# A graph layer on one core: message sums in plain fp32 over windows of 64 nodes, and VectorE adds the gathered rows and b_e in place of a stored table and ScalarE copies

## The chip, the cores and the metric

One core of a Trainium2 chip runs the whole kernel. The metric is the device time of a run in microseconds (us). The profile is one profiled execution of the same program.

## What is computed

A graph has 8192 nodes with 256 features (x) and 131072 edges with 64 attributes, sorted by destination. The parts that matter here:

```
ea  = edge_attr @ w_e + b_e                      # 131072 x 256
msg = relu(x[src] + ea)                          # rows of x gathered by src
agg = segment_sum(msg, dst, num_segments=8192)
h_local = relu((x + agg) @ w1 + b1) @ w2 + b2    # then a scale, a shift and a residual
attention over graphs of 32 nodes, 4 heads; out = h_local + h_attn
out = out + relu(out @ m_w1 + m_b1) @ m_w2 + m_b2; a layer norm ends it
```

## The kernel before, in words

**Turns.** The 131072 edges are 1024 tiles of 128; two tiles are a pair (512 pairs), four pairs a group (128 groups of 1024 edges). A turn handles two pairs, so there are 256 turns and three more at the end; eight turns, with four groups, go with one block of 256 nodes. Each of the engines PE (TensorE), DVE (VectorE), ACT (ScalarE), POOL (GpSimd) and SP (which issues most DMAs) has its own program, written out by hand turn by turn, with waits on semaphores between them; every engine works strictly in the order of its program. `heads_in` and `nodes_in` say which step of which block's attention and node layers falls into which turn.

**Gathers (L316 to L335).** POOL issues two indirect DMAs for each pair, 1024 in all. Each takes 128 indices from the SBUF tile `srcs` and brings 128 rows of 1 KB into `xg`, which has room for 8 pairs (NX). For the first 80 pairs (XB_PAIR) the rows come from x, and POOL may go as far as seven pairs are already copied (`s_seed`). From then on they come from `xb_dram`, a table of x + b_e, and POOL waits once every two pairs for the edge products (`s_prod`) of the turn three back. The table is made during the first 32 turns: SP loads a sixteenth of x, DVE adds b_e to it (`add_be`, L565, instruction at L569), and SP stores it.

**A pair's way.** ACT copies the two gathered tiles into one of four PSUM banks `EA` (`seed`, L354, copy at L360), after their landing (`s_xg`) and after the bank is free. PE adds the edge attributes times w_e on top (`products`, L728, matmuls at L746: 64 rows each, two pairs side by side in the two halves of the array's rows); for the first 80 pairs it also adds b_e by a matmul of ones with b_e split in two fp32r parts (L738). ACT makes the high half of the message, relu rounded to fp32r (`high`, L362, at L364); DVE makes the low half, relu minus the high half (`low`, L559, at L561).

**A group's way.** DVE makes a 128x128 0/1 matrix for each of the eight tiles of a group (`make_onehot`, L572, at L573): which of 128 nodes from the group's first one an edge goes to. PE multiplies it with both halves of the messages, 16 fp32r matmuls into bank `G` (`sum_group`, L752, at L761). ACT copies the sums out (`copy_agg`, L369), PE transposes them (L770), and DVE adds them to a window of 128 nodes in `aggT` (`add_agg`, L579, at L591). The window's start is loaded from `base_i` into a register.

**Order.** DVE's turn is: `low` of two pairs, in even turns `add_agg`, `add_be` and `make_onehot`, then attention and node steps. ACT's turn is: `seed` of the next turn's two pairs, `high` of this turn's, in odd turns `copy_agg`, then attention and node steps. PE's turn is `products`, in odd turns `sum_group`, in even turns the transposes, then attention and node steps (all plain matmuls of the dense layers are at L710). In two turns of eight a node step of DVE (L635, L653) waits for a product that PE makes late in the same turn. Other two-input additions and products of DVE on SBUF tiles are L618 and L677, in attention and in the layer norm.

Of the kernel before, what the change touches and what calls it, by code (L numbers as in the profile page):

```python
# [16 lines left out]
P = 128  # L17
TG = 8
# [13 lines left out]
XB = 16  # L32
XB_ROWS = N // XB // P
XB_PAIR = XB * PG + 16
# [3 lines left out]
PER = N // NG  # L38

# [24 lines left out]

EA_PE = XB_PAIR // PG + 1

# [18 lines left out]
def gnn_layer(nc, t, out):  # L86
# [5 lines left out]
    k.xb_dram = nc.dram_tensor("xb_dram", (N, C), fp32, kind="Internal").ap()  # L92
    with ExitStack() as ctx:
# [10 lines left out]
        k.ident, k.iota = sb("ident", [P, P]), sb("iota", [P, P])  # L104
# [5 lines left out]
        k.base_i, k.bad_i = sb("base_i", [P, P], i32), sb("bad_i", [P, 1], i32)  # L110
        k.lohi = sb("lohi", [P, 6])
# [4 lines left out]
        k.be_rows, k.be_hl = sb("be_rows", [P, C]), sb("be_hl", [P, C], f32r)  # L116
        k.be_ones = sb("be_ones", [P, P], f32r)
        k.xrow = sb("xrow", [P, 2, XB_ROWS, C])
# [6 lines left out]
        k.mh, k.ml = sb("mh", [P, NM, 2 * C], f32r), sb("ml", [P, NM, 2 * C], f32r)  # L125
        k.onehot = sb("onehot", [P, 2, TG, P], f32r)
# [26 lines left out]
def program(nc, k):  # L153
    t, EA, G, X = k.t, k.EA, k.G, k.X
    aggT, ident, vecT, s12 = k.aggT, k.ident, k.vecT, k.s12
    xg, ea, mh, ml, onehot = k.xg, k.ea, k.mh, k.ml, k.onehot
    with ExitStack() as ctx:
        def sem(name):
# [8 lines left out]
        s_xrow = [sem(f"s_x_part_{n}") for n in range(2)]  # L167
        s_xadd, s_xbst = sem("s_be_added"), [sem(f"s_xb_stored_{n}") for n in range(2)]
# [8 lines left out]
        s_be = sem("s_be_split")  # L177
        s_seed, s_prod, s_mh, s_ml = (sem(n) for n in ("s_x_seeded", "s_ea_product", "s_msg_high",
                                                       "s_msg_low"))
        s_seg, s_agg, s_aggT, s_added = (sem(n) for n in (  # L180
            "s_group_summed", "s_agg_copied", "s_agg_transposed", "s_agg_added"))
        s_oh = sem("s_onehot_made")
# [36 lines left out]
        def _(sp):  # L219
# [27 lines left out]

            xb_parts = k.xb_dram.rearrange("(m p r) c -> m p r c", p=P, r=XB_ROWS)
            x_parts = t["x"].rearrange("(m p r) c -> m p r c", p=P, r=XB_ROWS)

            def load_part(m):
                if m >= 2:
                    sp.wait_ge(s_xbst[m % 2], 16 * (m // 2))
                sp.dma_start(k.xrow[:, m % 2, :, :], x_parts[m, :, :, :]).then_inc(s_xrow[m % 2], 16)

            for m in range(2):
                load_part(m)
            for turn in range(TURNS):
# [3 lines left out]
                m = turn // 2  # L262
# [4 lines left out]
                if turn % 2 == 1 and 2 <= m + 1 < XB:  # L267
                    load_part(m + 1)
# [37 lines left out]
        def _(pool):  # L306
# [9 lines left out]
            for q in range(NP):  # L316
# [946 lines left out]
```

## Time and profile before

| | us |
|---|---|
| runs of the kernel before, median of 2 | 1602.03 (1601.25 to 1602.81) |
| profiled execution, first to last instruction (span) | 1362.1 |
| PE busy, of the span | 1284.3 |
| POOL busy, of the span | 982.0 |
| DVE busy, of the span | 860.7 |
| ACT busy, of the span | 804.9 |

The profile gives the profiled execution's span and no other time of it; the runs' median lies 239.9 us above that span. Busy times leave out register, branch, semaphore and DMA-issuing instructions, except that a gather on POOL counts as busy while POOL builds it. A fp32 matmul of the program stands as two instructions in the trace, an fp32r one as one.

### The profile page before, as it was taken

The page shows a single profiled execution, that of the slowest core. Times are in us where ns is not written, and L with a number is a line of the kernel's source. Part 1 is how long each engine was busy: PE and PEld are TensorE (multiplying, and loading weights), DVE is VectorE, ACT ScalarE, POOL GpSimd, SP SyncE. Part 2 cuts the span into 40 slices and gives each one's busy share as a digit, 9 for nine tenths or more (in the row PEclk, how much of TensorE's full clock was granted, in tenths as well). Part 3 has the DMA queues.
Part 4 walks back from the last instruction along what each step waited for, and adds up shares of the span by engine and source line. Part 5 has one row for each costly group of instructions (what it writes and reads, how often), then busy time and mean ns, then how long its engine had stood idle before and what let it go on. Part 6 is the DMA issues. An engine that isn't in the chain of part 4 may idle for free.

```text
span 1362.1 us, 22937 instructions
## 1 busy us (share of the span) xinstructions
PE 1284.3 (94%) x8410; PEld 1045.5 (77%) x8410; DVE 860.7 (63%) x1690; ACT 804.9 (59%) x1697; POOL 982.0 (72%) x1032
## 2 busy tenths in 40 slices
PE   5988999999999999999999999999999999999997
PEld 4777888777877777777777787777777777778776
DVE  3786676666566566566666666666666666566642
ACT  2555555665566566666666666666666666666652
POOL 7777774777777777777777777777777777777750
PEclk8999999999999999999999999999999999999999
DMA  9777764556445555545555545555554555554441
GB/s 345 237 242 248 238 215 126 170 167 174 141 146 171 174 163 174 157 131 170 175 170 171 167 143 154 175 174 167 175 158 138 168 175 172 169 161 148 138 120 32
DMA packets 109651, 232.93 MB, mean 171 GB/s; under 512 B 21985, under 2 KB 46817, under 8 KB 109537
## 3 DMA queue, kind: packets, MB, share of 16 engines
q0 software_dynamic: 49152, 134.28, 34.6%
q1 hardware_dynamic: 58944, 93.87, 20.5%
q10 hardware_dynamic: 1440, 3.29, 0.7%
q8 instruction: 67, 1.10, 0.3%
q14 instruction: 48, 0.39, 0.1%
HBM read 206.19 MB, written 25.17 MB: 170 GB/s over the span
## 4 chain that ended last, share of the span: by engine, by line
POOL 51%; PE 21%; issue 17%; DVE 6%; DMA 3%; ACT 1%; SPq 0%; DVEq 0%; POOLq 0%; ACTq 0%
POOL xg L331 51%; PE bank L761 5%; PE bank L710 5%; PE both L710 5%; PE bank L746 4%; DMA xg<-xb_dram,srcs 2%; DVE onehot L573 2%; DVE ml L561 1%; DMA aggT<-in_xT_dram 1%; DVE xrow L569 1%; PE bank L738 1%; ACT mh L364 1%; PE bank L849 1%; DVE aggT L591 0%; PE both L886 0%
## 5 line engine op out<-in xcount | busy, mean ns | idle before, releaser
L331 POOL DMA_INDIRECT xg<-xb_dram,srcs x864 | 820.4, 950 | 283.5 <-issue 258.3
L561 DVE SCALAR_TENSOR_TENSOR ml<-bank,mh 128x512 fp32r<-128x512 f32 x512 | 329.8, 686 | 308.3 <-ACT mh L364 305.7
L360 ACT COPY bank<-xg 128x512 f32<-128x512 f32 x512 | 301.5, 597 | 210.0 <-DMA xg<-xb_dram,srcs 167.7
L364 ACT ACTIVATE mh<-bank 128x512 fp32r<-128x512 f32 x512 | 277.5, 594 | 162.1 <-PE bank L746 160.5
L761 PE MATMUL bank<-mh,onehot 128*128 128x256 f32 x1024 | 266.2, 298 | 52.0 <-DVE onehot L573 52.0
L746 PE MATMUL bank<-we,ea 64*128 64x256 f32 x2048 | 290.0, 402 | 0.0
L761 PEld LDWEIGHTS bank<-mh,onehot 128*128 128x128 f32 x1024 | 196.7, 192 | 97.1 <-DVE onehot L573 77.5
L761 PE MATMUL bank<-ml,onehot 128*128 128x256 f32 x1024 | 253.1, 285 | 0.0
L746 PEld LDWEIGHTS bank<-we,ea 64*128 64x128 f32 x2048 | 177.7, 187 | 74.3 <-issue 30.3
L331 POOL DMA_INDIRECT xg<-in_x_dram,srcs x160 | 160.6, 1004 | 51.7 <-issue 43.6
L761 PEld LDWEIGHTS bank<-ml,onehot 128*128 128x128 f32 x1024 | 197.4, 193 | 0.0
L573 DVE TENSOR_TENSOR onehot<-bank,rel 128x1024 fp32r<-128x1024 f32 x128 | 155.6, 1215 | 0.0
L369 ACT COPY agg<-bank 128x256 f32<-128x256 f32 x128 | 47.7, 373 | 135.4 <-PE bank L761 135.4
L710 PE MATMUL both<-xT,iwT 128*128 128x256 f32 x512 | 123.8, 385 | 0.0
L710 PE MATMUL both<-m,h 128*128 128x256 f32 x496 | 117.3, 379 | 0.0
L710 PEld LDWEIGHTS both<-xT,iwT 128*128 128x128 f32 x512 | 92.4, 190 | 15.7 <-issue 5.0
L710 PEld LDWEIGHTS both<-m,h 128*128 128x128 f32 x496 | 89.5, 190 | 9.6
L635 DVE SCALAR_TENSOR_TENSOR h<-xT,s,bank 128x256 f32<-128x256 f32 x64 | 27.9, 477 | 108.5 <-PE bank L710 108.5
L710 PE MATMUL bank<-h,m 128*128 128x256 f32 x264 | 64.7, 389 | 1.7 <-DVE h L635 1.7
L710 PE MATMUL bank<-oT,owT 128*128 128x256 f32 x256 | 65.7, 379 | 0.0
L710 PE MATMUL bank<-h,w 128*128 128x256 f32 x256 | 65.5, 379 | 0.0
L710 PE MATMUL both<-iwT,xT 128*128 128x256 f32 x240 | 62.7, 384 | 0.0
(111 smaller groups left out, 1402.6 us busy)
## 6 DMA issues: line engine op xcount, KB each, us to landing
ea<-in_ea_dram SPq DMA_DIRECT2D x128, 256.0 KB, 3.9
xg<-xb_dram,srcs POOLq DMA_INDIRECT x864, 2.8
xT<-in_xT_dram SPq DMA_DIRECT2D x32, 256.0 KB, 3.6
aggT<-in_xT_dram SPq DMA_DIRECT2D x32, 256.0 KB
xrow<-in_x_dram SPq DMA_DIRECT2D x16, 512.0 KB, 6.3
xb_dram<-xrow SPq DMA_DIRECT2D x16, 512.0 KB, 3.2
oT_dram<-oT SPq DMA_DIRECT2D x32, 256.0 KB, 2.5
xn<-in_x_dram SPq DMA_DIRECT2D x32, 256.0 KB, 4.6
```

The source lines that it names most:

```text
L331: pool.indirect_dma_start(xg[:, q % NX, n * C:(n + 1) * C], None, t["x"] if q < XB_PAIR else k.xb_dram[:, :], bass.IndirectOffsetOnAxis(k. ...
L360: nc.scalar.copy(EA[q % 4][:, :], xg[:, q % NX, :]).then_inc(s_seed, 1)
L364: nc.scalar.activation(mh[:, q % NM, :], EA[q % 4][:, :], ACT.Relu).then_inc(s_mh, 1)
L369: nc.scalar.copy(k.agg[:, :], G[:, 0:C]).then_inc(s_agg, 1)
L561: nc.vector.scalar_tensor_tensor(ml[:, q % NM, :], EA[q % 4][:, :], 0.0, mh[:, q % NM, :].bitcast(fp32), ALU.max, ALU.subtract).then_inc(s ...
L569: nc.vector.tensor_tensor(part, k.be_rows[:, :].unsqueeze(1).to_broadcast([P, XB_ROWS, C]), part, ALU.add).then_inc(s_xadd, 1)
L573: nc.vector.tensor_tensor(onehot[:, n % 2, :, :], G[:, 2 * P:3 * P].unsqueeze(1).to_broadcast([P, TG, P]), k.rel[:, n, :].unsqueeze(2).to_ ...
L635: ins = nc.vector.scalar_tensor_tensor(k.o[:, c, :], k.xT[:, j % NXT, c, :], s12[:, 6 + c:7 + c], B[:, c * NB:(c + 1) * NB], ALU.mult, ALU ...
L710: ins = nc.tensor.matmul(to, stationary(c), moving(c), start=start and c == 0, stop=stop and c == blocks - 1, skip_group_check=skip)
L738: nc.tensor.matmul(EA[(2 * d + tile // 2) % 4][:, tile % 2 * C:(tile % 2 + 1) * C], k.be_ones[:, :], k.be_hl[:, :], start=False, stop=True ...
L746: ins = nc.tensor.matmul(EA[(2 * d + pair) % 4][:, two * C:(two + 1) * C], ea[rows, n % NEA, at:at + P], k.we[rows, :], start=False, stop= ...
L761: ins = nc.tensor.matmul(G[:, 0:C], onehot[:, n % 2, tile, :], half[:, q % NM, two * C:(two + 1) * C], start=tile == 0 and half is mh, sto ...
```

## The change

It takes out the table `xb_dram`, its loads, stores and additions, the split of b_e and its matmuls, and ACT's copies. DVE now adds gathered rows and b_e into the PSUM bank for all pairs, at the start of its turn. The message is one plain fp32 tile made by ACT. The sums are plain fp32 over windows of 64 nodes: a group's first four tiles go to the upper half of `G`, the last four to the lower half, each half with a window start of its own, and `add_agg` adds them one after the other. All gathers read x, and POOL waits by `s_prod` from the ninth pair on.

```diff
-XB = 16
-XB_ROWS = N // XB // P
-XB_PAIR = XB * PG + 16
+SUB = 2
+TS = TG // SUB
+W = P // SUB
...
-        k.mh, k.ml = sb("mh", [P, NM, 2 * C], f32r), sb("ml", [P, NM, 2 * C], f32r)
-        k.onehot = sb("onehot", [P, 2, TG, P], f32r)
+        k.msg = sb("msg", [P, NM, 2 * C])
+        k.onehot = sb("onehot", [P, 2, TG, W])
...
@@ POOL @@
-                if q == XB_PAIR:
-                    for n in range(2):
-                        pool.wait_ge(s_xbst[n], 16 * (XB // 2))
-                if NX <= q < XB_PAIR:
-                    pool.wait_ge(s_seed, q - NX + 1)
-                if q >= XB_PAIR and q % 2 == 0:
-
+                if q >= NX and q % 2 == 0:
                     pool.wait_ge(s_prod, q // 2 - 2)
...
-                        t["x"] if q < XB_PAIR else k.xb_dram[:, :],
+                        t["x"],
@@ ACT @@
-            def seed(q):
-                act.wait_ge(s_xg[q % NX], 32 * (q // NX + 1))
...
-                nc.scalar.copy(EA[q % 4][:, :], xg[:, q % NX, :]).then_inc(s_seed, 1)
-
-            def high(q):
+            def message(q):
                 act.wait_ge(s_prod, q // 2 + 1)
-                nc.scalar.activation(mh[:, q % NM, :], EA[q % 4][:, :], ACT.Relu
-                                     ).then_inc(s_mh, 1)
+                nc.scalar.activation(msg[:, q % NM, :], EA[q % 4][:, :], ACT.Relu
+                                     ).then_inc(s_msg, 1)
@@ DVE @@
-            def low(q):
...
-            def add_be(n):
...
+            def seed(q):
+                dve.wait_ge(s_xg[q % NX], 32 * (q // NX + 1))
+                if q == 0:
+                    dve.wait_ge(s_ber, 16)
+                    dve.wait_ge(s_set, 1)
+                if q >= 4:
+                    dve.wait_ge(s_msg, q - 3)
                 nc.vector.tensor_tensor(
-                    part, k.be_rows[:, :].unsqueeze(1).to_broadcast([P, XB_ROWS, C]), part, ALU.add).then_inc(s_xadd, 1)
+                    EA[q % 4][:, :].rearrange("p (a c) -> p a c", a=2),
+                    xg[:, q % NX, :].rearrange("p (a c) -> p a c", a=2),
+                    k.be_rows[:, :].unsqueeze(1).to_broadcast([P, 2, C]), ALU.add
+                ).then_inc(s_seed, 1)
...
             def add_agg(n):
-                at = nc.vector.value_load(k.base_i[0:1, n:n + 1], min_val=0, max_val=N - P)
+                at = [nc.vector.value_load(k.base_i[0:1, sub, n:n + 1], min_val=0, max_val=N - W)
+                      for sub in range(SUB)]
                 dve.wait_ge(s_aggT, n + 1)
-                if n == NG - 1:
+                if n:
                     dve.wait_ge(s_added, n)
...
+                sums = G[:, 0:C].rearrange("p (c n) -> p c n", n=P)
+                for sub in range(SUB):
+                    if sub:
+                        dve.wait_ge(s_half, n + 1)
+                    window = aggT[:, :, bass.ds(at[sub], W)]
+                    nc.vector.tensor_tensor(window, sums[:, :, sub * W:(sub + 1) * W], window,
+                                            ALU.add).then_inc(s_added if sub else s_half, 1)
...
-            add_be(0)
+            seed(0)
+            seed(1)
             make_onehot(0)
...
-                for q in (a, b):
+                for q in (a + 2, b + 2):
                     if q < NP:
-                        low(q)
+                        seed(q)
@@ PE @@
-                if 2 * d < XB_PAIR:
-                    for tile in range(4):
-                        nc.tensor.matmul(
-                            EA[(2 * d + tile // 2) % 4][:, tile % 2 * C:(tile % 2 + 1) * C],
-                            k.be_ones[:, :], k.be_hl[:, :], start=False, stop=True,
-                            skip_group_check=True)
...
             def sum_group(n):
-                if n == NG - 1:
-                    pe.wait_ge(s_ml, NP)
+                pe.wait_ge(s_msg, PG * (n + 1))
+                if n < NG - 1:
+                    pe.wait_ge(s_oh, n + 2)
+                else:
                     pe.wait_ge(s_added, n)
-                else:
-                    pe.wait_ge(s_oh, n + 2)
-                for tile in range(TG):
-                    q, two = PG * n + tile // 2, tile % 2
-                    for half in (mh, ml):
-                        ins = nc.tensor.matmul(G[:, 0:C], onehot[:, n % 2, tile, :],
-                                               half[:, q % NM, two * C:(two + 1) * C],
-                                               start=tile == 0 and half is mh,
-                                               stop=tile == TG - 1 and half is ml)
+                for tile in range(TS):
+                    for sub in range(SUB):
+                        at = sub * TS + tile
+                        q, two = PG * n + at // 2, at % 2
+                        ins = nc.tensor.matmul(G[sub * W:(sub + 1) * W, 0:C],
+                                               onehot[:, n % 2, at, :],
+                                               msg[:, q % NM, two * C:(two + 1) * C],
+                                               start=tile == 0, stop=tile == TS - 1)
```

The set-up on DVE loses the split of b_e and works out two window starts for each group in place of one; the softmax step 7 on DVE waits for ACT's exponentials in every block instead of the last one alone.

## Rows read from the trace of the kernel before

**Rows 1.** The page: an engine's busy time, and PE's granted clock in 40 slices.

```profile
PE 1284.3 (94%) x8410; PEld 1045.5 (77%) x8410; DVE 860.7 (63%) x1690; ACT 804.9 (59%) x1697; POOL 982.0 (72%) x1032
...
PEclk8999999999999999999999999999999999999999
```

**Rows 2.** The page: the chain that ended last, by engine.

```profile
POOL 51%; PE 21%; issue 17%; DVE 6%; DMA 3%; ACT 1%; SPq 0%; DVEq 0%; POOLq 0%; ACTq 0%
```

**Rows 3.** Waits of POOL: us in total, times, longest us.

```profile
POOL xg L331 <- PE bank L746: 25.1, 17, 11.9
POOL xg L331 <- ACT bank L360: 6.5, 16, 1.7
```

**Rows 4.** Groups of gathers: count, busy us, mean ns of one, idle before.

```profile
L331 POOL DMA_INDIRECT xg<-xb_dram,srcs x864 | 820.4, 950 | 283.5 <-issue 258.3 <-PE bank L746 25.1
...
L331 POOL DMA_INDIRECT xg<-in_x_dram,srcs x160 | 160.6, 1004 | 51.7 <-issue 43.6 <-ACT bank L360 6.5 <-DMA srcs<-in_srcs_dram 1.5
```

**Rows 5.** Timeline of POOL, first and last gathers: start us, duration us.

```profile
3.37 1.18 POOL L331 DMA_INDIRECT xg<-in_x_dram,srcs  x1 [1.53 <-DMA srcs<-in_srcs_dram]
4.86 0.95 POOL L331 DMA_INDIRECT xg<-in_x_dram,srcs  x1 [0.30 <-issue]
...
27.40 1.99 POOL L331 DMA_INDIRECT xg<-in_x_dram,srcs  x1 [0.30 <-issue]
...
1317.04 0.95 POOL L331 DMA_INDIRECT xg<-xb_dram,srcs  x1 [0.30 <-issue]
```

**Rows 6.** One block of eight turns by windows: length; PE, PEld, DVE, ACT, POOL busy; clock.

```profile
655.97:695.93 39.96, 38.77 (x257) 31.34 (x257) 25.96 (x52) 25.16 (x53) 30.46 (x32) 1.00 0.56 163
```

**Rows 7.** Timelines of gathers (POOL) and VectorE instructions that overlap them.

```profile
124.38 1.22 DVE L569 TENSOR_TENSOR xrow<-be_rows,xrow 128x1024 f32<-128x1024 f32 x1
124.58 1.84 POOL L331 DMA_INDIRECT xg<-in_x_dram,srcs  x1 [0.30 <-issue]
...
306.42 0.42 DVE L618 TENSOR_TENSOR dif<-dif,rs 128x256 f32<-128x256 f32 x1
306.55 1.11 POOL L331 DMA_INDIRECT xg<-xb_dram,srcs  x1 [0.30 <-issue]
...
652.09 1.21 DVE L573 TENSOR_TENSOR onehot<-bank,rel 128x1024 fp32r<-128x1024 f32 x1
652.19 0.95 POOL L331 DMA_INDIRECT xg<-xb_dram,srcs  x1 [0.30 <-issue]
```

**Rows 8.** Groups of VectorE: count, busy us, mean ns of one.

```profile
L561 DVE SCALAR_TENSOR_TENSOR ml<-bank,mh 128x512 fp32r<-128x512 f32 x512 | 329.8, 686 | 308.3 <-ACT mh L364 305.7
...
L573 DVE TENSOR_TENSOR onehot<-bank,rel 128x1024 fp32r<-128x1024 f32 x128 | 155.6, 1215 | 0.0
...
L591 DVE TENSOR_TENSOR aggT<-bank,aggT 128x256 f32 x128 | 54.4, 425 | 9.0 <-PE bank L770 6.6 <-issue 1.9
```

**Rows 9.** ACT's copies (L360) and what they waited for; gathers, issue to landing.

```profile
L360 ACT COPY bank<-xg x512: 576/590/632, 11.5 to 1321.2; 128x512 f32<-128x512 f32 x171
...
  DMA xg<-xb_dram,srcs: 167.7, 159
...
  DMA xg<-in_x_dram,srcs: 14.4, 4
...
xg<-xb_dram,srcs POOLq DMA_INDIRECT x864, 2.8
```

**Rows 10.** PE: timeline of one block, and the group of the b_e matmuls.

```profile
650.05 2.76 PE L710 MATMUL both<-xT,iwT 128*128 128x256 f32 x12
...
686.23 0.28 PE L761 MATMUL bank<-mh,onehot 128*128 128x256 f32 x1
686.35 0.28 PE L761 MATMUL bank<-ml,onehot 128*128 128x256 f32 x1
686.56 1.09 PE L849 MATMUL bank<-probT,vn 128*64 128x128 f32 x16
...
L738 PE MATMUL bank<-be_hl,be_ones 128*128 128x256 f32 x160 | 33.5, 334 | 13.5 <-ACT bank L360 13.5
```

More of the change, by code:

```diff
@@ L466, in settle @@
                 dve.wait_ge(s_own, made[0])
-            lo, hi, base, bad, span, off = (k.lohi[:, n:n + 1] for n in range(6))
+            lo, hi, base, bad, span, off = (k.lohi[:, n, :] for n in range(6))
+            even = k.even[:, 0:1].to_broadcast([P, SUB])
             dve.wait_ge(s_ident, 4)
-            step_of(nc.vector.tensor_copy(G[:, 2 * P:3 * P], k.iota[:, :]))
-            nc.vector.tensor_scalar(k.be_ones[:, :], ident[:, :], 0.0, None, ALU.mult)
+            step_of(nc.vector.tensor_copy(G[:, 2 * P:2 * P + W], k.iota[:, :]))
@@ L489, in _ @@
             settle()
             nc.vector.tensor_tensor(span, hi, base, ALU.subtract)
-            nc.vector.tensor_tensor(bad, lo, k.even[:, :], ALU.subtract)
-            step_of(nc.vector.tensor_tensor(off, base, k.even[:, :], ALU.subtract))
+            nc.vector.tensor_tensor(bad, lo, even, ALU.subtract)
+            step_of(nc.vector.tensor_tensor(off, base, even, ALU.subtract))
             settle()
-            nc.vector.tensor_scalar(span, span, float(P - 1), None, ALU.is_gt)
+            nc.vector.tensor_scalar(span, span, float(W - 1), None, ALU.is_gt)
@@ L495, in _ @@
             nc.vector.tensor_scalar(bad, bad, float(-PER * SLACK), None, ALU.is_lt)
-            step_of(nc.vector.tensor_scalar(off, off, float(AHEAD * NB - (GI - 1) * PER - P), None,
+            step_of(nc.vector.tensor_scalar(off, off, float(AHEAD * NB - (GI - 1) * PER - W), None,
                                             ALU.is_gt))
             settle()
-            step_of(nc.vector.tensor_tensor(bad, bad, span, ALU.max))
+            step_of(nc.vector.tensor_reduce(
+                k.bad[:, :], k.lohi[:, 3:6, :].rearrange("p a s -> p (a s)"), AX.X, ALU.max))
@@ L508, in _ @@
-            step_of(nc.vector.tensor_reduce(span, X[0][:, P:2 * P], AX.X, ALU.max))
+            for sub in range(SUB):
+                tiles = slice(sub * TS, (sub + 1) * TS)
+                ins = nc.vector.tensor_tensor(
+                    k.rel[:, :, tiles], k.dst_p[:, :, tiles],
+                    X[0][:, sub * P:(sub + 1) * P].unsqueeze(2).to_broadcast([P, NG, TS]),
+                    ALU.subtract)
+            step_of(ins)
+            nc.vector.tensor_copy(k.base_i[:, :, :].rearrange("p s n -> p (s n)"),
+                                  X[0][:, 0:SUB * P])
```

113 lines of the change are left out of this document (28 added, 85 removed).

## The prediction

> **What bounds the kernel now.** I read the page's busy shares first. PE is busy for 1284.3 us of 1362.1, at nearly full clock (2.4 GHz) but for the first slice [rows 1], and looks like the bound. The chain that ended last says otherwise: 51% of it is POOL, and a further 17% "issue", time between instructions [rows 2]. So I looked at POOL's gathers. There are 1024, each takes 0.95 us, and the next one starts 0.30 us after it although nothing is waited for; from 4.86 to 27.40 us there are 18 starts in a row, one every 1.252 us [rows 4, 5]. At that pace 1024 gathers need 1023 x 1.252 + 0.95 = 1282 us. The first starts at 3.37 and the last ends at 1317.99 us [rows 5], a stretch of 1314.6 us. The 32.6 us above the pace are: 25.1 + 6.5 us of waits for PE and ACT in 33 places, less the 33 x 0.30 us that are pace anyway, so 21.7 us [rows 3]; (1004 - 950) ns x 160 = 8.6 us of longer gathers in the first part [rows 4]; and 2.3 us scattered. After the last gather come 44.1 us of tail. POOL's queue of gathers is the bound, and at most 22 us can come from whatever POOL waits for. PE is the close second: a block of eight turns, 32 gathers, lasts 39.96 us, and PE is busy in 38.77 of them [rows 6].
>
> **Why some gathers are long** is the second thing to read, in the timelines [rows 7]. A gather that started at 124.58 took 1.84 us instead of 0.95. It started inside the addition of b_e at L569, which has two inputs in SBUF and ended at 125.60; the gather ended at 126.42, 0.82 later. The same at 306.55: the softmax product L618, two SBUF inputs too, ended at 306.84, and the gather at 307.66, again 0.82 later. The gather at 27.40 (1.99 us [rows 5]) is of this kind. The control is the gather at 652.19, inside a one-hot comparison that reads one input from PSUM and one from SBUF: 0.95 us, undisturbed. So about 0.13 us after its start a gather does something (0.95 - 0.82) that must wait until a two-SBUF-input instruction of DVE has ended.
>
> **Pricing that.** If such an instruction of length L stands at an arbitrary place in a pitch T of 1.25 us, it delays the gathers by L x L / 2T on average. For L569: 1.22 x 1.22 / 2.5 = 0.60 us each; the measured cost is 8.6 us over 16 additions, 0.54 us each. The formula holds to a tenth.
>
> **The change, part by part.**
> 1. DVE's new `seed` adds xg and be_rows, both in SBUF, 128x512, into PSUM, 512 times. The trace has no such shape; the 128x512 instruction at L561 takes 0.686 us [rows 8], and L569 with twice the elements 1.22 us, so I take 0.69. By the formula a seed at an arbitrary place costs the gathers 0.69 x 0.69 / 2.5 = 0.190 us. But a seed that waits for its rows is not at an arbitrary place: the rows land 2.8 us after the issue of the pair's second gather [rows 9], that is 0.3 us into the third pitch after it, past the sensitive 0.13 us, and the seed ends at 0.99, before the next start at 1.25. Those cost nothing. How many wait? ACT's copies, which stand at the same place of ACT's turn, did so 159 + 4 times of 512 [rows 9]; the other 349 came late. I take the same share: 349 x 0.190 = 66 us on POOL's path. Bounds: none delayed, 0; all at arbitrary places, 512 x 0.190 = 97 us.
> 2. The waits of POOL, 21.7 us, mostly go: the additions of b_e by PE (33.5 us busy for 160 instructions [rows 10]) leave the first 40 turns, where PE was the slower one, and the change of wait rule at pair 80, the single wait of 11.9 us [rows 3], no longer falls there. The stricter rule now holds from pair 8, and can cost at the start; I leave 5 us of waits, between 0 and 12.
> 3. The 16 additions at L569 go, and with them 8.6 us of long gathers.
> 4. Sums on PE. Sixteen fp32r matmuls follow each other at 0.12 us: 1.92 us a group. A plain fp32 one of the same size is two instructions of 0.216 us each ((2.76 - 0.38) / 11, twelve in a row). The eight new ones, 16 instructions, would be 3.46 us in a row. But they alternate between the halves of the output partitions as L849's do, and there 16 instructions of 128 columns took (1.09 - 0.28) / 15 = 0.054 us each, half of the 0.108 that such a stream needs alone [rows 10]. So 16 x 0.108 = 1.73 us; 0.2 us a group comes off PE, 0.8 of the 38.77 us of a block. It is hidden behind POOL: worth nothing but some 1 us in the tail.
> 5. DVE: 512 seeds for 512 `low` of the same length; the one-hot halves from 1.215 to about 0.69 us; the window addition of 0.425 us [rows 8] becomes two, each between 0.21 and 0.42, with a second register load and a wait between. Together DVE is some 0.2 us a group lighter. Off the path. ACT loses 512 copies of 0.59 us. Off the path as well, as are 32 transfers of 512 KB.
> 6. DVE is in order: in two turns of eight it stands before a product of PE (node steps at L635 and L653) and the next turn's seeds are queued behind it, so PE's next products but one wait. Written out over one block with these durations, PE's work is 38.0 us and about 1 us of waiting comes in; POOL's 40 us cover it. If the gathers were not there, it would be the bound.
>
> **A page against the change.** The Trainium skill, SBUF - State Buffer, "Who interferes with whom", says that a DVE instruction with two SBUF inputs contends with a GpSimd instruction that reads SBUF, and that the second to start blocks until the first is done. It agrees with [rows 7]: the gather reads its indices from SBUF. The same section infers that tensor_tensor does not hold up DMAs issued by GpSimd, because building descriptors needs the write interface only; by that the first term would be 0 and the time 1576 us. The 1.84 us gather speaks against it.
>
> **The sum**, against the span: start 3.4, pace 1282, scattered 2.3, seeds 66, waits 5, tail 43.1 = 1401.8 us, 39.7 us above 1362.1. The runs' median lies 239.9 us above the span; nothing in the trace says what that is, and I carry it over unchanged: 1602.0 + 39.7 = 1641.7 us, 2.5% slower. A measurement of this kernel tells about 2%, 32 us, from no change.
>
> **Rivals.** (a) Likeliest, 60%: late seeds hold up gathers, with between 40 and 95 us: 1615 to 1671 us, 1642 in the middle. (b) 25%, on the other side: the seeds hardly hold up gathers, because writing to PSUM makes them different or because nearly all of them fall in step with the landings once PE has slack. It decides from 26 us of delay downwards. With 0 to 26 us the time is 1602 - 26.3 + (0 to 26) = 1576 to 1602 us. For it: 163 copies already fell in step, and a slower POOL lets more do so. Against it: DVE has turns with over 3 us of attention work, after which its seeds are late whatever the landings do. (c) 5%: the two halves of the sum don't overlap. Then a group costs 1.54 us more, a block 38.77 + 6.2 = 45 us, and PE is the bound: 5 us x 32 - 20 = 140 us more, about 1742 us. (d) 10%: DVE's order becomes the bound, with 2 to 3 us for each block beyond POOL's pace on top of half of the delays: 1602 - 26 + 33 + 64 to 96 = 1673 to 1705 us. The clock could join in (d): with PE idle more often, stretches at the half clock (1.2 GHz) as in the first slice would appear.
>
> **How the numbers follow.** Slower by over 2% (above 1634): all of (c) and (d), and of (a)'s 0.60 some 0.42, since delays up to 58 us leave it below: 0.57. Within 2%: the other 0.18 of (a), and 0.20 of (b)'s 0.25: 0.38. Faster by over 2% (below 1570): 0.05, from (b), if the start also goes better than assumed. The range from 1580 to 1685 takes in the bounds 0 (nearly) and 97 of the seeds' delay and the nearer half of (d), and leaves out (c) and the ends.
>
> **What would show it.** Right: gathers with a mean of about 1.01 us, many of 1.1 to 1.6 us that started inside a seed and ended 0.82 us after it; hardly a wait on POOL; PE idle for 5% more of the span, waiting for seeds; sum matmuls that start every 0.108 us. Wrong: gathers of 0.95 us throughout (b); sum matmuls at 0.216 us (c); POOL waiting for PE in every block while PE waits for DVE (d); or a distance between span and median other than 240 us.

## The result and the profile after

The changed kernel takes 1575.58 us, the median of 2 runs (1575.54 to 1575.62), against 1602.03 us before. The ratio is 0.9838 with a 95% interval of 0.9808 to 0.9868: 1.6% faster. The forecast was 1642 us with a range of 1580 to 1685 us, so it had the wrong sign and the range missed.

The page of the changed kernel: busy shares and granted clock, then the chain that ended last by engine.

```profile
PE 1363.5 (87%) x8251; PEld 973.1 (62%) x8251; DVE 793.9 (50%) x1797; ACT 524.5 (33%) x1185; POOL 1025.5 (65%) x1032
...
PEclk8978999999999899999999999999999999999989
...
PE 38%; another core or an unknown queue 28%; ACT 10%; DVE 10%; issue 9%; POOL 2%; DVEq 2%; DMA 0%; SPq 0%
```

Beside [rows 1] and [rows 2] this is another regime, not the same one with a small edit. POOL had 51% of the chain before and has 2% now; 28% goes to waits whose releaser the profile cannot name. The span is 1573.9 us, only 1.7 us below the median of the runs, where it was 239.9 us below it before. Next, who waited (engine, line, waited for: us in total, times, longest), changed kernel:

```profile
ACT msg L324 <- remote: 461.0, 128, 6.1
POOL xg L299 <- issue: 273.6, 879, 1.0
POOL xg L299 <- remote: 151.4, 101, 2.3
POOL xg L299 <- PE bank L692: 71.9, 43, 3.2
```

```profile
707.83 1.14 PE L692 MATMUL bank<-we,ea 64*128 64x256 f32 x8
...
710.04 1.89 PE L662 MATMUL both<-h,m 128*128 128x256 f32 x8
...
712.21 1.08 ACT L324 ACTIVATE msg<-bank 128x512 f32<-128x512 f32 x2 [5.05 <-remote]
```

```profile
708.73 0.94 POOL L299 DMA_INDIRECT xg<-in_x_dram,srcs  x1 [0.30 <-issue]
709.97 0.95 POOL L299 DMA_INDIRECT xg<-in_x_dram,srcs  x1 [0.30 <-issue]
712.45 0.94 POOL L299 DMA_INDIRECT xg<-in_x_dram,srcs  x1 [1.53 <-remote]
```

The products end at 708.97. ACT, which needs nothing but them, begins at 712.21, 3.2 us later; POOL, which waits for the same semaphore, begins at 712.45. POOL had stopped at 710.92, and the update came 1.3 us after that. PE itself was not held up: it began further matmuls at 709.17, 710.04 and 711.86. Over all matmuls of this trace that raise a semaphore I set the time of the update against the end of the matmul, which the profile models: half of the recorded updates come more than about 2 us late, a tenth more than about 5 us. Nine tenths of the recorded updates of ACT and DVE come within 0.01 us in the same trace. In the profile of before, PE's come within 0.02 us.

So the 240 us between the profile of before and its runs were not time around the span. That profile is of an execution with PE's updates on time; the timed runs, as I infer from their times and from `e1_before` below, were of the other kind, with PE's updates late. Which kind it is seems to go with the chip: each of the first four sets of runs below was on one chip (9, 8, 5 and 11), and within a set all kernels were of one kind. The fifth was on two, 0 and 5, both of the kind with updates on time. Chip 5 is the only one that was seen twice.

### The profile page after: what moved, and what is told of

It reads as the page before. It is cut to its first block, busy times and chain, and to the rows that moved or that the text cites. A ratio compares the mean times of both kernels' runs of the same rounds, so it can differ in the third digit from the quotient of the medians.

```text
span 1573.9 us, 22965 instructions
## 1 busy us (share of the span) xinstructions
PE 1363.5 (87%) x8251; PEld 973.1 (62%) x8251; DVE 793.9 (50%) x1797; ACT 524.5 (33%) x1185; POOL 1025.5 (65%) x1032
## 4 chain that ended last, share of the span: by engine, by line
PE 38%; another core or an unknown queue 28%; ACT 10%; DVE 10%; issue 9%; POOL 2%; DVEq 2%; DMA 0%; SPq 0%
PE both L662 11%; PE bank L662 8%; PE bank L692 8%; PE bank L708 8%; ACT msg L324 5%; DVE bank L516 3%; POOL xg L299 2%; DVEq L530 2%; DVE onehot L523 1%; ACT h L333 1%; PE bank L717 1%; DVE mx L556 1%; DVE aggT L546 1%; ACT agg L329 1%
## 5 line engine op out<-in xcount | busy, mean ns | idle before, releaser
L299 POOL DMA_INDIRECT xg<-in_x_dram,srcs x1024 | 1024.5, 1001 | 498.5 <-issue 273.6
L324 ACT ACTIVATE msg<-bank 128x512 f32<-128x512 f32 x512 | 278.0, 596 | 719.5 <-remote 461.0
L692 PE MATMUL bank<-we,ea 64*128 64x256 f32 x2048 | 317.8, 418 | 92.0 <-DVE bank L516 59.0
L516 DVE TENSOR_TENSOR bank<-xg,be_rows 128x512 f32<-128x512 f32 x512 | 332.9, 695 | 64.6 <-DMA xg<-in_x_dram,srcs 36.8
L708 PE MATMUL bank<-msg,onehot 128*64 128x256 f32 x2048 | 272.8, 410 | 42.3 <-DVE onehot L523 33.1
L546 DVE TENSOR_TENSOR aggT<-bank,aggT 128x128 f32 x256 | 74.6, 291 | 371.8 <-remote 217.7
L708 PEld LDWEIGHTS bank<-msg,onehot 128*64 128x64 f32 x2048 | 157.1, 145 | 144.9 <-issue 73.8
L523 DVE TENSOR_TENSOR onehot<-bank,rel 128x512 f32<-128x512 f32 x128 | 87.1, 681 | 0.1
L717 PE MATMUL bank<-ident,agg 128*128 128x128 f32 x256 | 60.0, 319 | 27.2 <-ACT agg L329 14.4
L556 DVE TENSOR_REDUCE mx<-both 32x8 f32<-32x256 f32 x128 | 53.5, 418 | 30.8 <-remote 26.8
```

The costliest lines, as they stand in the source:

```text
L299: pool.indirect_dma_start(xg[:, q % NX, n * C:(n + 1) * C], None, t["x"], bass.IndirectOffsetOnAxis(k.srcs[:, at:at + 1], 0)).then_inc(s_x ...
L324: nc.scalar.activation(msg[:, q % NM, :], EA[q % 4][:, :], ACT.Relu).then_inc(s_msg, 1)
L516: nc.vector.tensor_tensor(EA[q % 4][:, :].rearrange("p (a c) -> p a c", a=2), xg[:, q % NX, :].rearrange("p (a c) -> p a c", a=2), k.be_ro ...
L523: nc.vector.tensor_tensor(onehot[:, n % 2, :, :], G[:, 2 * P:2 * P + W].unsqueeze(1).to_broadcast([P, TG, W]), k.rel[:, n, :].unsqueeze(2) ...
L546: nc.vector.tensor_tensor(window, sums[:, :, sub * W:(sub + 1) * W], window, ALU.add).then_inc(s_added if sub else s_half, 1)
L556: ins = nc.vector.tensor_reduce(k.mx[g, :], scores[g, :, g], AX.X, ALU.max)
```

## Experiments

### First set: is it the profile that differs, and which half of the change gains?

`e1_before` is the kernel before, unchanged. `e2_sums_alone` has the new sums and leaves table, copies and additions of b_e as before:

```diff
-                for tile in range(TG):
-                    q, two = PG * n + tile // 2, tile % 2
-                    for half in (mh, ml):
...
+                for tile in range(TS):
+                    for sub in range(SUB):
+                        at = sub * TS + tile
```

`e3_seeds_alone` is the other half: no table, no copies, DVE's seeds, and the old sums and message halves.

```diff
+                nc.vector.tensor_tensor(
+                    EA[q % 4][:, :].rearrange("p (a c) -> p a c", a=2),
+                    xg[:, q % NX, :].rearrange("p (a c) -> p a c", a=2),
+                    k.be_rows[:, :].unsqueeze(1).to_broadcast([P, 2, C]), ALU.add
...
-                nc.scalar.copy(EA[q % 4][:, :], xg[:, q % NX, :]).then_inc(s_seed, 1)
```

`e4_seed_one_sbuf_input` is the changed kernel with one SBUF input in the seed; it leaves out b_e and adds the old contents of the PSUM bank in its place:

```diff
-                    k.be_rows[:, :].unsqueeze(1).to_broadcast([P, 2, C]), ALU.add
+                    EA[q % 4][:, :].rearrange("p (a c) -> p a c", a=2), ALU.add
```

Expected:

> The kernel before, unchanged, profiled once more: its span of 1362.1 us and its median of 1602.0 us don't fit together, while the changed kernel's span (1573.9) and median (1575.6) do. Theory P (TensorE really works slower in timed executions than that one profile shows: in the profile of after, semaphores of PE come a median of 2.0 us after the modelled ends of its matmuls, in that of before 0.02 us): a new profile of before shows a span near 1600 us with such late semaphores and POOL waiting for PE in many places. Theory O (240 us lie outside the span of before, and only of before): the span is 1362 us again. Time 1602 us in both.

> The change's message sums alone (plain fp32 messages, windows of 64 nodes, no low halves on DVE); ACT's copies and the table of x + b_e stay. Theory P (TensorE is the bound in timed executions, and the new sums are a little cheaper for it): most of the gain of 26 us, 1575 to 1585 us. Theory G (POOL's gathers are the bound): no gain from the sums, 1595 to 1605 us.

> The change's seeding alone: DVE adds gathered rows and b_e into the banks for all pairs, no table, no copies by ACT; messages stay split in high and low halves, with 16 fp32r matmuls a group. DVE now makes seeds and low halves. Theory P: PE loses only the b_e matmuls of 40 turns (33.5 us busy), 1575 to 1600 us, and late gathers are hidden. Theory G: gathers held up by seeds cost 40 to 97 us less the 30 us of waits that go, 1615 to 1670 us.

> The changed kernel, but the seed's second input is the PSUM bank that it writes instead of be_rows in SBUF (so b_e is left out and the bank's old sums are added): an instruction of the same size and length with one SBUF input. Both theories: gathers of 0.95 us, no long ones but those beside L571 and L630. Theory P: the time stays within 5 us of the changed kernel's 1575.6, since the delays lie beside waits for PE. Theory G: 40 to 60 us faster.

| run | us | ratio to before, 95% | span |
|---|---|---|---|
| e1_before | 1640.64 (before: 1638.38) | 1.0025 (0.998 to 1.007) | 1627.5 |
| e2_sums_alone | 1623.53 | 0.9909 (0.9875 to 0.9944) | 1627.4 |
| e3_seeds_alone | 1592.39 | 0.9731 (0.9627 to 0.9835) | 1587.6 |
| e4_seed_one_sbuf_input | 1604.04 | 0.9802 (0.9702 to 0.9903) | 1600.1 |

The kernel before, profiled again, has a span of 1627.5 us, and the same face as the changed kernel's page (who waited, e1_before):

```profile
POOL xg L331 <- issue: 270.0, 865, 1.6
POOL xg L331 <- PE bank L746: 143.2, 78, 10.7
POOL xg L331 <- remote: 121.7, 59, 2.5
POOL xg L331 <- ACT bank L360: 61.3, 21, 7.3
```

[rows 3] had 25.1 and 6.5 us in the places of the last three rows. All kernels of this set, the unchanged one included, are slower than in the first comparison, so ratios are set against each other here, and not times; in microseconds e1, e2 and e4 lie above what was expected. The half with the seeds (and without the table) gains 2.7%, the sums alone about 1%. With one SBUF input in the seeds the long gathers are gone (0.5 us beyond 0.95 us each, over all 1024), and nothing is gained by it here: e4 is not faster than e3. The changed kernel itself is not in this set.

### Second set: order on ACT, and POOL's rule of waiting

`e5_after` is the changed kernel. `e6_copy_agg_later` tests whether ACT's order is what holds up the seeds of before, `e7_gathers_by_seed` lets POOL run on by the seeds and not by the products, `e8_seeds_alone_again` repeats e3.

```diff
-                if turn % 2 == 1 and 3 <= turn <= 2 * NG + 1:
-                    copy_agg(turn // 2 - 1)
+                if turn % 2 == 0 and 4 <= turn <= 2 * NG + 2:
+                    copy_agg(turn // 2 - 2)
```

```diff
-                    pool.wait_ge(s_prod, q // 2 - 2)
+                    pool.wait_ge(s_seed, q - NX + 2)
```

Expected:

> The changed kernel, unchanged, on the same chip as the three others of this call, so that they can be set against it and not only against before. All theories: ratio to before near 0.984 (0.975 to 0.99). If the sums had been the larger part of the gain it would be clearly below the seeds-alone kernel of this call (theory S); theory Q (it is ScalarE's order, seeds queued behind copy_agg, that the change removes) has it equal to or above that kernel.

> The kernel before, with one edit in ScalarE's order: copy_agg of a group, which waits for PE's sum_group of the same turn, comes one turn later, behind the seeds of that turn, so that no seed is queued behind it. Theory Q (in timed executions PE's semaphores come late, ACT stands 445 us in front of copy_agg, and seeds, so products, wait behind it): most of the change's gain without the change, ratio 0.975 to 0.99. Theory S (the gain comes from the work that goes from PE: b_e matmuls and fp32r sums): 1.00 within 0.5%. Theory G (POOL is the bound): 1.00.

> The changed kernel, with POOL's wait put on the seed that frees the buffer (pair q-7) instead of the edge products of three turns back: gathers may run two pairs farther ahead. If late PE semaphores let POOL run dry so that DVE waits for rows (theory G in its timed form), the time falls by 10 to 40 us. If PE's own chain is the bound and POOL's waits are only slack (theory Q), less than 5 us either way.

> The seeds-alone kernel once more (DVE seeds, sums as before in fp32r halves), on the same chip as the changed kernel. Theory Q: ratio to before 0.97 to 0.985 as the first time (0.973), and not slower than the changed kernel, so the sums bring nothing on top. Theory S: clearly slower than the changed kernel, by 10 us or more.

| run | us | ratio to before (1625.76), 95% | span |
|---|---|---|---|
| e5_after | 1588.64 | 0.9757 (0.9717 to 0.9797) | 1586.6 |
| e6_copy_agg_later | 1626.02 | 0.9997 (0.9979 to 1.0015) | 1631.1 |
| e7_gathers_by_seed | 1810.44 | 1.1106 (1.1037 to 1.1175) | 1815.5 |
| e8_seeds_alone_again | 1584.16 | 0.9721 (0.9676 to 0.9766) | 1583.9 |

PE's updates were late here too. ACT's order is not it (e6). The changed kernel (e5) is no faster than the seeds alone (e8), so the new sums bring nothing on top of the seeds. e7 missed every expectation and taught most. POOL now often runs for 15 to 21 us without a stop, where it ran for 10, and PE's updates come later still, up to 12 us. Timeline of e7, PE, then ACT, then POOL:

```profile
823.57 1.95 PE L708 MATMUL bank<-msg,onehot 128*64 128x256 f32 x16
...
837.56 0.69 PE L717 MATMUL bank<-ident,agg 128*128 128x128 f32 x2 [8.19 <-ACT agg L329]
```

```profile
837.14 0.37 ACT L329 COPY agg<-bank 128x256 f32<-128x256 f32 x1 [10.29 <-remote]
```

```profile
836.39 0.95 POOL L299 DMA_INDIRECT xg<-in_x_dram,srcs  x1 [0.30 <-issue]
847.45 0.95 POOL L299 DMA_INDIRECT xg<-in_x_dram,srcs  x1 [10.11 <-DVE bank L516]
```

The sum ends at 825.52; ACT's copy of it, which waits for nothing later of PE, begins at 837.14, 11.6 us after, when POOL is at the last gather of its run. Then PE, ACT and DVE run through what had piled up, and POOL waits 10.1 us. So on such a chip, while gathers follow each other without a pause, PE's updates wait. By place in the run the medians of e5 are 0.02 us for matmuls that end in the time of the first two gathers, then 2.4 and 4.6 to 5.1 us, and falling towards the pause (4.3, 3.3, 2.2, 1.4), as updates that are let go together would. After the last gather of a kernel all are on time again. What in the chip holds them, no run shows.

### Third set: fewer gathers in flight

The guess was that gathers in flight hold PE's updates. `e9_two_in_flight` and `e12_three_in_flight` let POOL issue a gather only when the one two, or three, before it has landed; `e11_before_two_in_flight` is e9's edit on the kernel before; `e10_shorter_lead` makes POOL wait for the products of one turn later.

```diff
...
+                    done = at - 2
+                    if done >= 0:
+                        pool.wait_ge((s_xg, s_xh)[done % 2][done // 2 % NX],
+                                     16 * (done // 2 // NX + 1))
...
```

```diff
-                    pool.wait_ge(s_prod, q // 2 - 2)
+                    pool.wait_ge(s_prod, q // 2 - 1)
```

Expected:

> The changed kernel, with one pacing wait on POOL: a gather starts only when the gather two before it has landed, so at most two are in flight (each half of a pair gets its own semaphore for that). Theory H (while gathers follow each other without a pause, PE's semaphore updates are held, from about the third gather on, and come 1 to 2 us after the run of gathers stops; so POOL's wait for PE costs 185 to 285 us in pauses): PE's updates come within 0.1 us in nine of ten cases, pauses for PE vanish, and the time is set by landings of 2.75 to 3.1 us for two gathers, 3.4 + 512 x (2.85 to 3.2) + 45 = 1510 to 1690 us. Theory N (PE itself runs late, whatever POOL does): the updates stay late, a median over 1 us, and the time rises above 1700 us.

> The changed kernel, POOL's wait one turn tighter (s_prod of two turns back in place of three): runs of gathers get shorter. Theory H: held updates are held for a shorter time (longest 6 us in place of 10), but POOL pauses more often, so 1560 to 1680 us; the opposite step, two pairs more of lead, cost 11%, so lead is no cure. Theory N: less lead costs POOL what PE's lateness of 2 us times 256 turns can make it, over 1700 us.

> The kernel before, with the same pacing wait (at most two gathers in flight). Theory H: the same holds there: PE's updates on time, POOL's pauses of 284 us gone, 1500 to 1690 us, and within 2% of the changed kernel paced the same way. Theory N: slower than 1700 us.

> The changed kernel, at most three gathers in flight. Landings of 2.75 to 3.1 us are mostly over when three starts of 1.25 us have passed, so this paces only behind slow landings. Theory H, if what holds the updates is the number of gathers in flight: some updates on time, 1480 to 1580 us. If it is the run of POOL's instructions without a pause that holds them, nothing changes: 1570 to 1600 us. Theory N: no change.

| run | us | ratio to before (1361.14), 95% |
|---|---|---|
| e9_two_in_flight | 1904.30 | 1.400 (1.3938 to 1.4062) |
| e10_shorter_lead | 1472.14 | 1.0823 (1.0757 to 1.0889) |
| e11_before_two_in_flight | 1897.98 | 1.3954 (1.3867 to 1.404) |
| e12_three_in_flight | 1488.13 | 1.094 (1.0903 to 1.0977) |

On this chip the kernel before runs in 1361.14 us, as long as its first profile: PE's updates are on time in every kernel of the set, so the set says nothing on the guess. Three of the four times were not expected: e9 and e11 lie over 200 us above the ranges for updates on time, and e10 lies 88 us below its own. e12 lies in a range, but no update was late that its limit could have freed. What the set does say is what two terms cost. A gather lands 3.1 us after its issue in e9 (the median), and with two in flight there is one per 1.82 us (1024 of them from 3.3 to 1862.0 us) instead of 1.25. And POOL's lead over PE is just enough: one turn less of it, and POOL waits for PE 127.1 us in 110 places (e10).

```profile
POOL xg L299 <- issue: 278.7, 913, 0.5
POOL xg L299 <- PE bank L692: 127.1, 110, 3.6
```

A turn is 4 x 1.25 = 5.0 us of gathers. So updates that come 2 to 4 us late take most of a turn from the lead, and could cost in the same way. That is argued, not shown, and it is not all: in e7 POOL had more lead, and the kernel was slower for it.

### Fourth set: repeats, and three in flight where updates are late

Expected of `e13_after_again`, `e14_one_sbuf_input_again` (e4's edit), `e15_seeds_alone_third` and `e16_three_in_flight_again` (e12's kernel):

> The changed kernel, unchanged. The chips differ: on two of them the kernel before takes 1626 and 1638 us with PE's semaphore updates a median of 1 to 2 us late, on a third it takes 1361 us with none late (0.02 us). If this call falls on a chip without late updates (kernel before near 1361 us): my forecast's mechanism (theory C: seeds with two SBUF inputs hold up gathers on POOL's path, which is the bound there) says 1361 + 40 = 1400 us, 1385 to 1432, slower by 2 to 5%; rival (b) of the forecast says 1335 to 1361. If it falls on a chip with late updates: ratio 0.972 to 0.987 once more.

> The changed kernel, with the seed's second input in PSUM (b_e left out, the bank's old sums added). Without late updates, theory C: gathers of 0.95 us, and faster than the changed kernel of this call by 40 to 75 us, so near 1335 us, 2% below before. With late updates: within 15 us of the changed kernel, since the delays lie inside pauses that POOL has anyway.

> Seeds by DVE, sums in fp32r halves as before. Without late updates, theory C: as slow as the changed kernel or slower by up to 40 us, since DVE makes both seeds and low halves and more seeds are late: 1395 to 1440 us. With late updates: within 10 us of the changed kernel, as the second time (1584 against 1589).

> The changed kernel with at most three gathers in flight. Without late updates: 1480 to 1495 us as before (1488), slower than the unpaced one by its pauses of 108 us. With late updates, theory H (a run of gathers without a pause holds PE's updates until they have landed): if gathers in flight hold them, updates come on time and the time falls to 1480 to 1560 us; if it is the run of instructions, 1570 to 1610 us.

| run | us | ratio to before (1628.63), 95% | span |
|---|---|---|---|
| e13_after_again | 1592.54 | 0.977 (0.9739 to 0.9801) | 1591.9 |
| e14_one_sbuf_input_again | 1589.71 | 0.9762 (0.9691 to 0.9834) | 1580.9 |
| e15_seeds_alone_third | 1586.31 | 0.9735 (0.9707 to 0.9763) | 1584.6 |
| e16_three_in_flight_again | 1619.04 | 0.9942 (0.9918 to 0.9967) | 1611.1 |

Updates are late on this chip. With three in flight they still are (about 1.6 us in the median, against about 2.2 in e13): a limit of three does not cure it, and the guess stands unsupported. Its rival, that the run of instructions holds them, gave 1570 to 1610 us, and 1619.04 is outside that too. e14 again gains nothing clear from undisturbed gathers (0.969 to 0.983 against 0.974 to 0.980 for e13). e15, the seeds alone, is again as fast as the changed kernel.

### Fifth set: the forecast's own case

> The changed kernel once more, for a chip without late updates. If the kernel before takes about 1361 us in this call: theory C says 1375 to 1405 us. The terms come from the kernel with three gathers in flight on such a chip: 3.3 to the first gather, 1282 of pace, 47 of long gathers, 45 of tail, and between 0 and 25 us of waits for PE. Rival (b) of the forecast says 1335 to 1361 us. If it falls on a chip with late updates: ratio 0.972 to 0.987 again.

> The changed kernel with the seed's second input in PSUM (b_e left out), for a chip without late updates, where the changed kernel takes 1373.6 us against 1359.8. Theory C (long gathers are on POOL's path there): no long gathers, and 25 to 45 us faster than the changed kernel, 1330 to 1350 us, a ratio to before of 0.98 to 0.99. If long gathers were hidden there too: ratio 1.005 to 1.015. If the call falls on a chip with late updates: ratio 0.97 to 0.985 as the two times before.

| run | us | ratio to before, 95% | span |
|---|---|---|---|
| e17_after_third (the changed kernel) | 1373.58 (before: 1359.76) | 1.0096 (1.003 to 1.0163) | 1371.9 |
| e18_one_sbuf_input_third (e4's edit) | 1336.27 (before: 1358.35) | 0.9827 (0.9779 to 0.9875) | 1334.3 |

Updates on time. Now the change is slower, by 1.0% (0.3 to 1.6), just under the range of 1375 to 1405 us, and the page looks like that of before, with POOL in the chain (e17: busy, chain, the gathers' group as out<-in, count, busy, mean ns, idle before; then who waited):

```profile
PE 1262.9 (92%) x8251; PEld 927.4 (68%) x8251; DVE 807.2 (59%) x1797; ACT 532.0 (39%) x1185; POOL 1011.8 (74%) x1032
...
POOL 61%; issue 20%; PE 11%; DMA 5%; DVE 2%; DVEq 0%; SPq 0%; ACT 0%
...
L299 POOL DMA_INDIRECT xg<-in_x_dram,srcs x1024 | 1010.9, 987 | 316.0 <-issue 306.8
```

```profile
POOL xg L299 <- PE bank L692: 7.6, 16, 2.0
```

The same group in e18, where the seeds have one SBUF input:

```profile
L299 POOL DMA_INDIRECT xg<-in_x_dram,srcs x1024 | 970.8, 948 | 316.9 <-issue 308.6
```

1010.9 - 970.8 = 40.1 us of longer gathers, and the spans differ by 37.6 us: this is what the second SBUF input costs when POOL is the bound. The two runs were on two chips, 0 and 5, but the kernel before takes 1359.76 and 1358.35 us there, so the chips account for little of it. The collision itself, in the timelines of e17, DVE and then POOL:

```profile
606.41 0.69 DVE L516 TENSOR_TENSOR bank<-xg,be_rows 128x512 f32<-128x512 f32 x1
608.66 0.70 DVE L516 TENSOR_TENSOR bank<-xg,be_rows 128x512 f32<-128x512 f32 x1 [1.56 <-DMA xg<-in_x_dram,srcs]
```

```profile
606.33 0.94 POOL L299 DMA_INDIRECT xg<-in_x_dram,srcs  x1 [0.30 <-issue]
607.58 0.95 POOL L299 DMA_INDIRECT xg<-in_x_dram,srcs  x1 [0.30 <-issue]
608.83 1.34 POOL L299 DMA_INDIRECT xg<-in_x_dram,srcs  x1 [0.30 <-issue]
```

The seed at 608.66 ends at 609.36, and the gather that began inside it ends at 610.17, 0.81 us later. This seed had waited 1.56 us for its rows. The seed at 606.41 began 0.08 us after the gather at 606.33, ran beside it, and cost nothing.

## Where the gain came from

With updates late, what does the change gain? The first comparison says 26 us, e5 and e13, against before on their own chips, 37 and 36. The count of gathers by stage tells where (from:to, length, POOL busy and instructions, granted clock, DMA share, GB/s). The count of the first stage includes 8 instructions of POOL's set-up. First e1_before, then the changed kernel, then e14:

```profile
0.00:300.00 300.00, 173.52 (x180) 0.86 0.58 189
400.00:900.00 500.00, 314.66 (x333) 0.96 0.46 139
900.00:1400.00 500.00, 315.20 (x333) 0.96 0.46 136
```

```profile
0.00:300.00 300.00, 201.12 (x208) 0.90 0.50 153
400.00:900.00 500.00, 336.57 (x338) 0.95 0.47 141
900.00:1400.00 500.00, 336.91 (x337) 0.95 0.46 137
```

```profile
0.00:300.00 300.00, 186.67 (x204) 0.89 0.49 152
400.00:900.00 500.00, 316.15 (x336) 0.93 0.46 139
900.00:1400.00 500.00, 316.32 (x335) 0.93 0.45 137
```

From 400 to 1400 us the kernels are alike: 666, 675 and 671 gathers (e3: 666, e13: 665), one per 1.48 to 1.50 us, although a gather takes 1.00 us in the changed kernel and 0.945 in the other two. POOL issues four or eight gathers, stops for the late update, and goes on; a longer gather shortens the stop. What sets the 1.49 us was not found: the chain of the changed kernel has 38% on PE and 28% on waits without a name. The gain lies in the first 300 us: a count of 208 (e3: 205, e13: 206) instead of 180.

Kernels are best set against each other on one chip. On chip 9, e3 has 25 more gathers than e1 by 300 us, and 25 x 1.49 = 37 us; its span is 39.9 us shorter. On chip 8, e6, whose edit of the kernel before changed nothing, stands for before (first row), and the changed kernel is e5 (second row):

```profile
0.00:300.00 300.00, 170.34 (x177) 0.86 0.58 188
```

```profile
0.00:300.00 300.00, 197.12 (x204) 0.89 0.50 152
```

27 more gathers are 40 us, and the spans, 1631.1 and 1586.6, differ by 44.5. For the 26 us of the first comparison itself there is no such pair, since its profile of before has the updates on time. e2, which keeps the table, has 186.

The first 300 us are the stage of the first 80 pairs: there the kernel before adds b_e on PE, stores its table, and POOL waits by ACT's copies, 61.3 us in 21 waits, and then 10.75 us in one when it changes over (who waited before 300 us, e1_before; the one after the change):

```profile
POOL xg L331 <- ACT bank L360: 61.3, 21, 7.3
POOL xg L331 <- issue: 48.2, 147, 1.6
POOL xg L331 <- PE bank L746: 13.4, 3, 10.7
```

```profile
282.06 0.95 POOL L331 DMA_INDIRECT xg<-xb_dram,srcs  x1 [10.75 <-PE bank L746]
```

The changed kernel waits 42.0 us for PE in the same stage (26.7 us in 16 "remote" rows, 15.3 in 8). So POOL waits for others 42.0 us there, where it waited 61.3 + 13.4 = 74.7 us before. Which of the things removed there (PE's additions, the copies, the stores, the old rule of waiting) gives how much was not separated. The place of copy_agg in ACT's order is not it: e6 moved that, and comes to 177.

## Why the prediction was wrong

**The step that failed** is "I carry it over unchanged". The 239.9 us between span and median were taken for a constant outside the kernel. They were inside: in e1_before the same kernel has a span of 1627.5 us with late updates of PE, of which the profile of before had none. With them POOL's pace is not the bound, so the forecast added its delays to a path that did not set the end. The last sentence of the prediction named the sign of it: a distance between span and median other than 240 us. It is 1.7.

**The pace as the bound** (1282 us) is right for the execution profiled, and wrong for those timed: there a gather comes every 1.49 us.

**Part 1, seeds that hold up gathers.** The mechanism was right, by place and by time: the gather ends 0.81 us after the seed in e17, 0.82 in [rows 7]. What the Trainium skill says in SBUF — State Buffer, "Who interferes with whom", of two SBUF inputs and a gather that reads SBUF agrees; its inference that tensor_tensor does not hold up DMAs from GpSimd does not: e17 and e18 differ by 37 us through that input alone.

The size was off. In e17, 123 gathers that began inside a seed were longer than the usual 0.95 us by 0.05 us or more, 0.31 us each, 38.3 us in all; the forecast had 66. Two assumptions were wrong, and their errors partly offset each other.

- Seeds that wait for their rows were to cost nothing. There were 206 of them (the DVE line of who waited, below), not 163, and seeds that had waited account for 48 of the long gathers and 14.6 us. The seed at 608.66 above is one.
- The others were to cost 0.190 us each, by L x L / 2T. They cost the remaining 23.7 us, 0.077 each for 306. The formula leaves out the 0.13 us that the prediction itself had read: a gather is held up only where the seed has more than that left. With it the estimate is (0.69 - 0.13) x (0.69 - 0.13) / 2.5 = 0.125 us each, which leaves 44 us of the 66. The comparison with L569 could not tell the two apart: with the 0.13 us the estimate is 0.48, without it 0.60, and 0.54 was measured. Why it is 0.077 in e17 and not 0.125 stays open.

The 0.13 us are no moment at which a gather stops and waits, as the prediction read them: then the seed at 606.41, 0.08 us behind its gather, would have held it up. The order of the starts decides. In the twelve traces with such seeds, all 1360 gathers that began 0.05 to 0.50 us into a seed (and met no second one) were held up; of 231 gathers with a seed that began in their first 0.12 us, none was.

```profile
DVE bank L516 <- DMA xg<-in_x_dram,srcs: 270.2, 206, 4.0
```

With updates late, gathers beyond 0.95 us add up to 56 to 68 us in the changed kernel (its first profile, e5, e13), and cost the kernel nothing that e4 and e14 could show.

**Parts 2 and 3, waits and long gathers of the first 80 pairs that go.** Right place. In e17 POOL's idle time is 316.0 us, of which 1023 x 0.30 = 306.9 are pace, so 9 us of waits are left; the forecast had 5, between 0 and 12. Where updates are late this stage is worth 37 to 40 us, not the 25 that the forecast took off.

**Part 4, the sums.** Right, the overlap of the halves above all. In the timeline of the changed kernel sixteen take 1.95 us, (1.95 - 0.38) / 15 = 0.105 us each; the forecast had 0.108:

```profile
737.45 1.95 PE L708 MATMUL bank<-msg,onehot 128*64 128x256 f32 x16
```

Rival (c) is out. Worth nothing on POOL's path, as said; 0.9% in e2 where updates are late.

**Parts 5 and 6, DVE.** The seed takes 0.695 us, forecast 0.69; the one-hot 0.681, forecast 0.69; a window addition 0.291, inside its bounds. DVE's order does not bind: in e17 POOL waits for PE for 7.6 us in 16 places. Rival (d) is out.

**The sum**, where it can be tested: 1401.8 us forecast for the span, 1371.9 measured in e17. The 28 us of the seeds' term are nearly all of it. In the runs: +13.8 us against a forecast of +39.7. **Rival (b)** gave 1576 to 1602 us, and 1575.58 lies at its edge; so does the 1576 us that goes with the inference of the Trainium skill. Both are luck. Seeds do hold up gathers, by 38.3 us in e17, and the gain of the first stage, which both took for some 26 us, is 37 to 40 us where updates are late.

No run here shows a kernel that computes everything and is faster than the one before where updates are on time: e18 leaves out b_e, and the seeds alone (e3) were never run on such a chip.

## What to carry to other kernels

When the profiled span and the timed runs are 15% apart, the profile is not of what is timed: profile the unchanged kernel again, before pricing anything, until one fits. Where a queue runs ahead of its consumer by a fixed lead, ask what a lag of a few microseconds in the consumer's signal does to it; three turns of lead were just enough here without any lag, and more lead was no cure where the lag was (e7). And a DVE instruction that shares its time with indirect gathers is cheaper with its second input in PSUM where the gathers are the bound: 37 us of 1374 here. When you price such a collision, ask which of the two starts first, count only what the gather really loses, and don't take an instruction for harmless because it waited.

## What was not expected of the hardware

- On some chips the semaphore updates of PE come late while indirect gathers follow each other: about 2 us in the median of the changed kernel's profile, up to 12 us in e7. On others they come within 0.02 us. The kernel before takes 1602 to 1638 us on the first kind (1602 in the first comparison) and 1358 to 1361 us on the second. The runs from e1 to e18 fell on five chips, three of the first kind (9, 8, 11) and two of the second (5, 0). The cause is open; that the updates come while POOL pauses, or at the end of its run, is seen in the traces; no intervention freed them.
- The traces of the two kinds differ in one more thing: where updates are late, many records of updates are missing. The same changed kernel has 587 updates of ACT, 925 of DVE and 6035 steps of DMA landings on record in its first profile, and 971, 1385 and 21132 in e17. So the lateness is measured on those that were recorded. Each run from e1 on has a recorded span, and whether the recording itself has a part in the lateness was not tested.
- Where updates are late the granted clock is lower, 0.938 for the changed kernel against 0.984 in e17, with PE idle more often; in e7 it is 0.879. Idle time of PE goes with it and not the lateness as such: in e9, with updates on time, a gather every 1.82 us and PE busy for 76% of the span, it is 0.873.
- A 128-row gather of 1 KB rows lands 2.8 us after its issue (before; 2.7 in e18), and a limit of two in flight costs 1.82 us for each (e9) where POOL alone needs 1.25.
